# A fused decoder layer: tables of their own for SyncE's transfers and for GpSimd's scatters and gathers

## The reference

```
x = x + attn(layernorm(x))                       # 16 heads, latent keys = values of width 72, causal
x = x + sigmoid(layernorm(x)) * wkv(ctx)         # two-way RWKV scan over each context batch
x = x + moe(layernorm(x))                        # 2048 tokens, 8 experts, 2 of them for each token

# attn:  Wdkv = x @ latent_w + latent_b ; q = x @ Wd_w[h] + Wd_b[h]
#        y = softmax(causal(q Wdkv^T / 4)) Wdkv ; return concat(y) @ out_w + out_b
# wkv:   ek = exp(k) ; A, B = sums of ek*v and ek over the past, decayed by exp(w)
#        (Af + Ab + exp(u+k) v) / (Bf + Bb + exp(u+k))
# moe:   logits = x @ router_w.T ; two experts and weights by a masked softmax
#        out[token] += weight * ((silu(x @ w_gate[e].T) * (x @ w_up[e].T)) @ w_down[e].T)
```

## Time and profile before

| | |
|---|---|
| median of 3 runs | 597.67 us (597.42 to 598.23) |
| profiled execution | span 602.4 us (its only time) |
| PE busy | 524.7 us, 87% |
| DVE, ACT, POOL busy | 363.1, 329.2, 314.9 us |
| TensorE's granted clock | 0.9 or more of full speed in most slices, 0.5 to 0.9 in those from 301 to 407 us |
| moved by DMA | 75.65 MB, 126 GB/s on average |

### The profile page before, as it was taken

One profiled execution on the slowest core, in us unless ns is written; L12 is line 12 of the kernel. 1 busy time (PEld: TensorE's weight loads), 2 busy tenths in 40 slices (PEclk: granted clock), 3 DMA queues, 4 the chain that ended last, 5 costly groups with the idle time before them and its releaser, 6 DMA issues.

```text
span 602.4 us, 10421 instructions
## 1 busy us (share of the span) xinstructions
PE 524.7 (87%) x3490; PEld 455.9 (76%) x3490; DVE 363.1 (60%) x749; ACT 329.2 (55%) x944; POOL 314.9 (52%) x277
## 2 busy tenths in 40 slices
...
GB/s 189 166 3 123 58 65 101 57 72 87 57 96 102 65 59 66 105 77 70 64 26 91 111 140 226 124 96 83 280 154 287 210 238 228 235 253 358 176 27 0
DMA packets 53087, 75.65 MB, mean 126 GB/s; under 512 B 10185, under 2 KB 41674, under 8 KB 52778
## 3 DMA queue, kind: packets, MB, share of 16 engines
...
## 4 chain that ended last, share of the span: by engine, by line
PE 39%; DMA 22%; issue 12%; DVE 9%; POOL 9%; ACT 4%; SPq 3%; POOLq 1%; another core or an unknown queue 0%; ACTq 0%
DMA out<-Y,TK 14%; PE P L672 10%; PE PO L796 8%; PE P L750 6%; PE P L768 5%; DMA qT<-qP 3%; POOL out L1717 3%; PE P L758 3%; DMA zP<-ZT 2%; SPq L577 2%; POOL cxa L1690 2%; ACT EB L1011 2%; POOL xs L1676 1%; DMA arena<-wd 1%; PE P L743 1%
## 5 line engine op out<-in xcount | busy, mean ns | idle before, releaser
L1011 ACT ACTIVATE EB<-P,small 128x128 f32<-128x128 f32 x256 | 90.7, 369 | 79.3 <-DVE small L1235 60.1
L1633 POOL TENSOR_TENSOR EB<-EB,small 128x512 f32<-128x512 f32 x64 | 78.9, 1241 | 98.4 <-DVE small L1239 98.2
L672 PE MATMUL P<-GT,WF 128*128 128x256 f32 x768 | 100.8, 290 | 7.2 <-DVE GT L1162 2.6
L672 PEld LDWEIGHTS P<-GT,WF 128*128 128x128 f32 x768 | 96.4, 196 | 8.2 <-DVE GT L1162 3.1
L1717 POOL DMA_INDIRECT out<-Y,TK x39 | 67.4, 1729 | 66.3 <-DMA out<-Y,TK 28.9
L768 PE MATMUL P<-PT,V 128*72 128x512 f32 x128 | 68.7, 619 | 11.2 <-ACT PT L1016 10.1
L750 PEld LDWEIGHTS P<-KT,qT 72*128 72x128 f32 x512 | 67.7, 194 | 12.6 <-DMA qT<-qP 6.8
L750 PE MATMUL P<-KT,qT 72*128 72x128 f32 x512 | 68.9, 278 | 5.4 <-DMA qT<-qP 4.7
L796 PE MATMUL PO<-Ow,zP 128*128 128x256 f32 x270 | 71.2, 407 | 2.0 <-DMA zP<-ZT 1.9
L1250 DVE COPY ZT<-P 72x512 f32<-72x512 f32 x64 | 43.3, 677 | 45.1 <-PE P L768 42.1
L796 PEld LDWEIGHTS PO<-Ow,zP 128*128 128x128 f32 x270 | 52.9, 205 | 17.2 <-issue 10.7
...
## 6 DMA issues: line engine op xcount, KB each, us to landing
...
```

The source lines that it names most:

```text
L672: r = e.matmul(o, lt(a), rt_(b), start=start and n == 0, stop=stop and n == 2, skip_group_check=skip)
L1011: e.activation(EB[i][:, j, :], S[:, 128 * j:128 * j + 128], ACT.Exp, bias=NM[i][:, j:j + 1], accum_out=SM[i][:, j:j + 1]).then_inc(s_exp, 1)
L1633: e.tensor_tensor(EB[i][:, :, :], EB[i][:, :, :], SM[i].unsqueeze(2).broadcast_to([128, 4, 128]), ALU.mult).then_inc(s_prob, 1)
```

## The change

Each engine gets a table of its own (`SYNC_STEPS`, `TENSOR_STEPS`, `VECTOR_STEPS`, `SCALAR_STEPS`, `GPSIMD_STEPS`), which lists only the steps in which it has a part, and walks it instead of `ORDER`. `ORDER` stays for the semaphore counts. The tables of PE, DVE and ACT have the order of the common table, so their instructions stand as before. SyncE's and GpSimd's tables have another order. No operation is added or removed. All lines behind the tables are 102 higher than before (L1633 is now L1735).

```
+SYNC_STEPS = """
...
+    Y.17 Y.19 Y.21 q.4.0 ctx.3 Y.23 q.4.1 q.4.2 q.4.3 q.4.4 Y.25 Y.27 Y.29 q.5.0 q.5.1 xd.0.0.4 q.5.2 Y.31 Y.33 q.5.3 q.5.4 q.6.0 Y.35 Y.37 Y.39 Y.40
...
+def steps_of(table):
+
+    return [(name, *map(int, a)) for name, *a in (w.split(".") for w in table.split())]
...
-    order = [(name, *map(int, a)) for name, *a in (w.split(".") for w in STEPS.split())]
+    order = steps_of(STEPS)
...
-            for name, *a in ORDER:
+            for name, *a in steps_of(SYNC_STEPS):
...
-            for s in ORDER:
+            for s in steps_of(GPSIMD_STEPS):
```

More of the change, by code:

```diff
@@ L182 @@
 """
+SYNC_STEPS = """
+    ctx.0 ctx.1 q.1.0 q.1.1 q.1.2 q.1.3 q.1.4 Y.1 Y.3 Y.5 q.2.0 q.2.1 Y.7 q.2.2 Y.9 ctx.2 q.2.3 q.2.4 Y.11 Y.13 q.3.0 q.3.1 q.3.2 Y.15 q.3.3 q.3.4
+    Y.17 Y.19 Y.21 q.4.0 ctx.3 Y.23 q.4.1 q.4.2 q.4.3 q.4.4 Y.25 Y.27 Y.29 q.5.0 q.5.1 xd.0.0.4 q.5.2 Y.31 Y.33 q.5.3 q.5.4 q.6.0 Y.35 Y.37 Y.39 Y.40
+    q.6.1 q.6.2 q.6.3 Y.41 q.6.4 Y.42 Y.43 Y.44 q.7.0 q.7.1 out.0.0.4 Y.45 Y.46 Y.47 out.1.0.4 q.7.2 Y.48 xd.1.0.4 q.7.3 Y.49 Y.50 q.7.4 Y.51 Y.52
+    Y.53 Y.54 Y.55 Y.56 Y.57 Y.58 Y.59 owh xd.2.0.4 xd.3.0.2 ltk.3 ltk.4 lw.2.0 lw.1.0 xd.3.2.2 lw.1.2 lw.1.1 lw.2.1 lw.3.0 out.2.0.4 out.3.0.2
+    out.3.2.2 lw.2.2 lw.3.1 lw.4.1 lw.5.1 lw.4.0 ltk.5 ltk.6 lw.3.2 lw.5.0 lw.6.0 ltk.7 ltk.8 lw.4.2 ltk.9 lw.6.1 lw.7.1 lw.5.2 lw.7.0 ltk.10 ltk.11
+    lw.6.2 lw.8.0 lw.9.0 ltk.12 ltk.13 lw.8.1 lw.9.1 ltk.14 lw.10.0 lw.7.2 lw.8.2 lw.9.2 lw.11.0 lw.10.1 lw.11.1 lw.10.2 lw.12.0 lw.13.0 lw.12.1
+    lw.13.1 lw.11.2 lw.12.2 ltk.15 ltk.16 ltk.17 lw.13.2 lw.14.1 lw.14.0 lw.15.0 lw.14.2 lw.15.1 lw.17.1 lw.15.2 lw.16.2 ltk.18 ltk.19 ltk.20 lw.17.0
+    lw.16.0 lw.18.0 lw.16.1 lw.18.1 lw.17.2 lw.18.2 lw.19.2 ltk.21 lw.19.0 lw.20.0 lw.20.2 lw.21.2 lw.22.2 ltk.22 lw.19.1 lw.20.1 lw.21.1 lw.21.0
+    lw.22.0 lw.22.1
```

86 lines of the change are left out of this document (84 added, 2 removed).

## The result

The changed kernel takes 632.77 us (median of 4 runs, 630.02 to 634.38) where the kernel before takes 597.54: the ratio is 1.0573 (95% interval 1.0534 to 1.0611), 34 us slower. I had forecast 596.3, in a range of 591.5 to 602.5. The forecast was wrong in sign and in size.

The account below looks back on a forecast made before the run. The last third was taken as bound by the chain of scatter-adds into `out`, not TensorE alone. Terms: -0.8 ahead of the experts, 0 for the links, -0.6 in the tail, -1.4 in all: 597.67 to 596.3 us, range 591.5 to 602.5.

Parts of the forecast that it names:

- five moves of stage 1: Attention: q.3.4 -1.5, stores of units 7 and 9 -1.0, scatter blocks +0.9 and +0.8, xb 0 and 1 0; together -0.8 us.
- The blocks of scatters: GpSimd, attention: six slot scatters ahead of N.52, +0.9 us (0 to +2.2); twelve ahead of N.60, +0.8 (+0.6 to +4.3).
- q.3.4: SyncE, attention: query load issued ahead of ctx 3 and unit 17's stores shortens PE's 2.51 wait; -1.5 us (0 to -2.5).
- Units 7 and 9: SyncE, attention: their stores move ahead of the loads they stood behind; at most -2.0 us, taken -1.0.
- SyncE in stage 2: Late weight thirds of tiles 3 to 5 hidden by the products' 6.7 us: cost 0, or 1 to 4 uncovered.
- The price of a link: Stage 2 scatter-add chain: gathers ahead, not load alone, lengthen a link; 7.6 us without them, 9.2 behind; links' sum 0.
- rival C: Stage 2: all gather-free links take 6.7 us, -3.6 on top of -1.4; 592.7 us, or 591.7; chance 0.19.
- Forecast links: Stage 2: times from one tile's scatter-add issue to the next; tile 13 at 540.1 against 540.06 before, so taken as 0.
- a sign of being wrong: Stage 2 chain: the prediction called itself wrong if gather-free links are 9 us or more.
- Rival B: Stage 2: gather batches exposed, loads set landings, gather-free links stay at 9.2 us; +5.4, 601.7 us; chance 0.26.

Follow-up runs that it names:

- e10: Kernel before with GpSimd's new order in stage 1, except the slot scatters, which keep their old places; ratio to before 1.024.
- e2: Changed kernel with SyncE's new table only, GpSimd in the common order; 608.5 us, ratio to before 1.018.
- e14: Kernel before with one swap in SyncE's order: query load q.1.4 ahead of the packing of unit 1; ratio 1.007.
- e18: Kernel before with one GpSimd step moved: rs.1.2 behind normalizations N.10 and N.11; ratio 0.998.
- e9: Kernel before with only GpSimd's blocks of slot scatters, six ahead of N.52 and twelve ahead of N.60; ratio 1.011.
- e3: Kernel before with GpSimd's new order in stage 1 only, SyncE in the common order throughout; ratio 1.045.
- e11: Kernel before with one place of SyncE's table changed: q.3.4 ahead of the packing of unit 17, ctx.3 later; ratio 0.997.
- e16: Kernel before with SyncE moves: q.3.4 early, slot tables 8 to 10 early, packings Y.7 and Y.9 ahead of q.2.2 and ctx.2; ratio 1.000.
- e7: Kernel before with SyncE's new order in stage 2 only, GpSimd's as before; ratio 0.995.
- e12: Kernel before with one SyncE change: slot tables 8 to 10 loaded right behind lw.6.0; ratio 0.995.
- e13: Kernel before with one swap in GpSimd's order: wa.0.1 ahead of normalization N.12; ratio 1.000.
- e15: Kernel before, but from tile 4 on each weight load of a big tile moves only half of its third; ratio 0.993.
- e8: Kernel before with both new tables, SyncE's and GpSimd's, in stage 2 only; ratio 1.018.

## Why the prediction was wrong

**The step that failed first: what was summed.** The sum had five moves of stage 1. GpSimd's table had moved some thirty steps there (`w6`, `w7`, `wa`, `rs`, `xb` against `N`), and SyncE's a dozen packings against query loads; I priced two places of the one and two of the other and took the rest as nothing, without naming what hid it. That rest is most of the loss: e10 (GpSimd without blocks) 9.9 us at unit 63, and of SyncE's 12.8 us at unit 45 (e2) the jumps of 4.0 at units 4 to 6 (5.3 in e14), 4.1 at unit 28, 2.0 at unit 38 and 3.7 at unit 45. Of these moves e14 and e18 show one each by itself.

**The blocks of scatters**, "+0.9" and "+0.8", measured 3.8 and 5.0 (e9), together 8.2 at unit 60 by e3 against e10. N.52 ended when I had said (314.24, against 295.9 + 18.2), but I let its lateness be overlapped by waits behind it; it went through the buffer of `EB` to unit 55 instead, with PE idle 2.25 and 1.27. Even my upper bounds, 2.2 and 4.3, were too low, if nearer than the values that I took.

**q.3.4**, "-1.5": 2.0 gained (e11, and the changed trace between units 18 and 21). Right.

**Units 7 and 9**, "-1.0": the gain is there (1.2) and is followed by a loss of 4.7 that I had not looked for, of the query loads behind the packings (e16).

**SyncE in stage 2**: the late weight thirds cost nothing that the times show, as said (e7, which has them, gains 0.5%, as e12 does without them), and early tables remove the wait of 9.5 us (e7, e12). But I did not carry the gain on: the sum had tile 3 at 452.5, e12 has it at 435.4, 12.8 us ahead of e13, which is its equal at unit 45. At the last scatter-add 7.4 of them are left in the traces, and 3.2 in the times (0.5%), since behind the early start the links of tiles 4 to 6 are 10.4, 9.1 and 9.1 in place of e13's 6.5, 7.1 and 8.8, and from tile 6 on the chain is about as far ahead as its products. How much of the loss is the load's and how much the products' pace was not separated. (e13's profiled execution, 601.67, was also its longest, so the 7.4 flatter e12.)

**The price of a link**, "7.6 without gathers ahead, 9.2 behind them", is the step that failed in stage 2. I took 4.93 against 6.37 us of landing at DMA shares of 0.88 and 0.90 as proof that load was not the cause. The earlier trace rows have 216 and 271 GB/s beside those shares: the load did differ, in the column that I did not read. I also read in the earlier trace rows that the products set most of the short links (rival C), from waits put down to `Y`; the chain that ended last has landings there (465.97 + 4.00 = 469.97 ahead of 470.81). The Trainium skill, DMA: Bandwidth & Descriptors, section "Queues, rings and completion order", says that a DMA engine takes turns between the rings of different queues; I had read it as a reason why only GpSimd's own transfers count. e15 and the table above speak for the plainer reading: SyncE's loads take their turns too, and the landing stretches with them. Forecast links against measured: 3 to 4, 7.6 and 6.5; 4 to 5, 11.6 and 12.3; 5 to 6, 9.2 and 10.0; 6 to 7, 9.0 and 9.5; 7 to 8, 9.2 and 11.6; 8 to 9, 7.6 and 6.8; 9 to 10, 7.6 and 11.1; 10 to 11, 9.0 and 10.7; 11 to 12, 9.2 and 8.3; 12 to 13, 7.6 and 9.5. Of the four links without gathers two are short and two are 9 or more, which I had named as a sign of being wrong. Rival B had the right mechanism for stage 2 (batches exposed, loads set a landing) but too low a price: +5.4, of which 0.7 was PE's, against 9.9 in the traces and 13.6 by the times (e8 against e7). It counted three links without gathers where the list has four, and kept the forecast's terms for stage 1, so that B, at 601.7, was 31 us short too.
